# First attention with rows loaded already turned, its mean folded into the query weights and its body in another order

## The chip, the cores and the metric

The kernel runs on one core of a Trainium2 chip. The metric is the device time of one execution in microseconds (us). A core has five engines with a queue of their own each: TensorE (PE; its weight loads are listed as PEld), VectorE (DVE), ScalarE (ACT), GpSimd (POOL) and SyncE (SP, which here only issues DMAs). They meet through semaphores alone.

## The reference, cut

2048 rows of 512 numbers (32 sequences of 64) go through four blocks, each added to x:

```python
x = x + L0_xattn(layernorm(x), ctx)        # the block that the change touches
x = x + L0_ffn(layernorm(x))               # sparse FFN
x = x + L1_xattn(layernorm(x), ctx, mask)
x = x + L1_ffn(layernorm(x))
# L0_xattn(text, features):
features_n = rmsnorm(features, fn_w)
Q = rmsnorm(text @ Wq.T + bq, qn_w)
K = rmsnorm(features_n @ Wk.T + bk, kn_w)
attn = softmax(Q @ K.T / sqrt(512))        # over the 64 keys of the same sequence
attended = attn @ features_n
```

## The kernel before, in words

The first attention (`l0_attention`) works on 16 tiles of 128 rows (`NT = 16`, `P = 128`); a tile holds two sequences, and `off` masks the other one's keys. `D = 512` lies in `KD = 4` blocks of 128. Each product is made of three fp32r ones, since every operand is split into a high and a low half (`split_mm`, L72, L73, L74): ScalarE writes the high half as a cast, and VectorE or GpSimd subtracts it from the original for the low one. A projection is thus 12 products of 512 columns, the scores 12 of 128, and the attend product 3 of 512.

Before and beside the tiles, the same function prepares the sparse FFN: maxima, scales and splits of its weights w1 and w2 (`w1_largest` in tiles 1 to 4, `scale_w1` and `split_w1` in tiles 7 to 14, `w2_largest`), the small factors c1 and c2 (`split_c1`, `split_c2`), and the layer norm, transposes and splits of the FFN's first 512 rows (`NORM_AT`, `PREP_AT`: one part in each of tiles 11 to 14).

Nothing is scheduled by a planner. Each engine has a list of steps of its own (`sp_steps`, `pool_steps`, `act_steps`, `dve_steps`, `pe_steps`): a hand-written prologue, and then `run`, which calls that engine's `body(n)` for n = 0 to 15. `body(0)` has `first`, `body(14)` lacks `ahead` (nothing of tile n+2), `body(15)` lacks `project` too. An engine executes its list strictly in order, and each step waits for semaphores.

A tile goes through these steps; the lines are those of the kernel before:

- SyncE loads x (L297), the context already turned (`cT_raw`, L302) and the context's rows (`craw`, L307).
- VectorE takes the mean and variance of the rows (L631, L635). GpSimd makes reciprocal square roots: in the prologue by L370 and L372, from then on three at once in `tile_roots` (L391, L393; L397 makes the shift -mean/std). ScalarE normalises the rows (L495). TensorE turns them (L808, four transposes into `bxT`), ScalarE casts the high half (L505), VectorE subtracts for the low half (L639).
- GpSimd weighs the context by `fn_w` (`weigh`, L365), ScalarE casts it (L501) and GpSimd subtracts (`features_lo`, L402). Of the turned context ScalarE casts the high half (L511), and GpSimd subtracts (`features_T`, L407).
- TensorE projects keys and queries. VectorE adds their biases (`key_bias`, L644; `query_bias`, L648); ScalarE squares and sums them (L519, L527; L486 for the context). `key_root` on GpSimd gives `krs`, and VectorE scales the keys into `kn` (`scale_keys`, L652).
- TensorE turns queries (L832) and keys (L838); ScalarE casts, VectorE subtracts (`qk_T`, L656 and L658). Then come the scores, VectorE's scaling with mask (L677) and the row maximum (L679), ScalarE's exponential with the denominator (L570), TensorE's transpose of the probabilities (L891), their split (L577, L691), the attend product, and VectorE's division and residual (`attended`, L664; the reciprocal is L687).

In the trace many of these buffers show as parts of `a_wide` (`xn`, `cw`, `kn`, `qb`, `kb`, the raw turned context) and `a_big` (all high and low halves). TensorE's `body(n)` is: both projections of tile n+1, scores of n, row transposes of n+2, attend of n-1, query and key transposes of n+1, (FFN rows,) probability transpose of n. On GpSimd `body(n)` has this piece, whose wait L423 is spoken of below:

```python
            if project:
                key_root(n + 1)
                pool.wait_ge(s_kn, n + 2)
            ...
            if project:
                features_lo(n + 1)
            if ahead:
                weigh(n + 2)
```

In the last tile TensorE also has products of the FFN's c1 as filler. The FFN's own products follow from 177.84 us on (L1336 and L72 to L74 with `xT_hi`; VectorE's L1213 to L1231, GpSimd's L1082, L1089 and L1095 belong to it). The two later blocks are not touched.

Of the kernel before, what the change touches and what calls it, by code (L numbers as in the profile page):

```python
# [21 lines left out]
ALU = mybir.AluOpType  # L22
# [162 lines left out]
def l0_attention(nc, ctx, big_ctx, m, prep, fw, a):  # L185
# [9 lines left out]
    bq_bank, bk_bank, bxT, b_prep, bqT, bkT, b_s, b_att = m.bank  # L195
    b_pT = b_s[:, P:2 * P]
# [9 lines left out]
    wide = sb("wide", [P, 7 * D])  # L206
    xn, cw, kn, qb, kb = (wide[:, n * D:(n + 1) * D] for n in range(5))
# [17 lines left out]
    nmx, den, rden = sb("nmx", [P, 1]), sb("den", [P, 1]), sb("rden", [P, 1])  # L225
# [14 lines left out]
    x_in, c_in_, cT_in = sem("x_in"), sem("ctx_in"), sem("ctxT_in")  # L240
# [16 lines left out]
    w2_in, s_w2m = [sem("w2_in0"), sem("w2_in1")], sem("w2_max_steps")  # L257

# [16 lines left out]
    LOAD_AT = {2: 2, 3: 3, 4: 0, 5: 1, 10: 2, 12: 3}  # L275
# [17 lines left out]
    def sp_steps(sp):  # L293
# [14 lines left out]

# [2352 lines left out]
```

## Time and profile before

| | us |
|---|---|
| three runs | 1509.44, 1509.60, 1510.46 (median 1509.6) |
| profiled execution, its own time | 1511.27 |
| span of that execution in the trace | 1509.5 |
| TensorE busy | 1463.2 (97%) |
| VectorE busy | 1127.8 (75%) |
| ScalarE busy | 795.1 (53%) |
| GpSimd busy | 710.3 (47%) |
| first attention, up to the FFN's first product | 177.84 |

All times in the text are of the one profiled execution. "Granted clock" is the share of full speed that TensorE was allowed in a stretch. A tile's stretch in the first attention runs from the first product of one key projection to that of the next: the projection of tile 2 begins at 48.25 us, and the stretch from there is called tile 2.

### The profile page before, as it was taken

To read this page: it belongs to the slowest core of one execution; us is meant where nothing else is said; L and a number is where in the kernel's file an instruction comes from. 1 tells how busy PE (TensorE), PEld (TensorE's weight loads), DVE (VectorE), ACT (ScalarE), POOL (GpSimd) and SP (SyncE) were. 2 spreads that over 40 slices of the span, in tenths; PEclk is the share of its full clock that TensorE was granted. 3 is DMA by queue.
4 is the path that set the end of the run, shared out by engine and by line. 5 is a ranking of instruction groups with operands and counts; after the bars stand their busy time and mean duration, and the time that the engine had idled before them with its cause. 6 is when DMAs were issued, how large, how long until landed. Compare 5 with 4: busy or idle time off the path is not lost.

```text
span 1509.5 us, 27579 instructions
## 1 busy us (share of the span) xinstructions
PE 1463.2 (97%) x9895; PEld 846.4 (56%) x9895; DVE 1127.8 (75%) x2172; ACT 795.1 (53%) x3201; POOL 710.3 (47%) x668
## 2 busy tenths in 40 slices
PE   5999999999999799999999999999999999999998
PEld 4888745555555455555555555555565555555554
DVE  5788787878876888776776676677677677667868
ACT  5678841211223576556546654754664565565763
POOL 5668875454565353334334343433434333343553
PEclk9999999999999999999999999999999999999999
DMA  7454435333344565653553554455445445334622
GB/s 248 147 175 136 123 81 126 98 77 50 65 88 72 117 147 84 110 119 64 100 105 53 95 88 81 86 87 95 81 80 105 79 73 103 64 60 67 99 50 112
DMA packets 358936, 146.87 MB, mean 97 GB/s; under 512 B 342304, under 2 KB 342688, under 8 KB 356112
## 3 DMA queue, kind: packets, MB, share of 16 engines
q1 hardware_dynamic: 357504, 137.77, 45.1%
q10 hardware_dynamic: 1296, 7.34, 1.5%
q8 instruction: 78, 1.28, 0.4%
q14 instruction: 58, 0.48, 0.1%
HBM read 58.02 MB, written 4.19 MB: 41 GB/s over the span
## 4 chain that ended last, share of the span: by engine, by line
PE 55%; DVE 5%; ACT 3%; DMA 1%; POOL 1%; issue 1%; SPq 0%; DVEq 0%; POOLq 0%; ACTq 0%
PE bank L72 18%; PE bank L74 17%; PE bank L73 17%; PE bank L2439 3%; ACT a_prob L1836 2%; DMA a_pT_lo<-a_p_lo 1%; POOL a_prob L1707 1%; DVE a_oT_lo L2106 1%; DVE x_res L2193 1%; DVE a_qve L2045 1%; ACT a_oT_lo L1813 0%; DVE a_p_lo L2094 0%; DVE a_nmx L2082 0%; DVE a_qr_lo L2035 0%; POOL a_xr_lo L1731 0%
## 5 line engine op out<-in xcount | busy, mean ns | idle before, releaser
L1836 ACT ACTIVATE a_prob<-a_prob,a_nmx 128x64 f32<-128x64 f32 x512 | 170.2, 334 | 183.7 <-DVE a_nmx L2082 183.7
L72 PE MATMUL bank<-w,a_oT_hi 128*128 128x512 f16 x512 | 194.0, 379 | 1.8 <-DVE a_oT_lo L2106 0.9
L74 PE MATMUL bank<-w,a_oT_hi 128*128 128x512 f16 x512 | 194.0, 379 | 0.0
L73 PE MATMUL bank<-w,a_oT_lo 128*128 128x512 f16 x512 | 194.0, 379 | 0.0
L72 PE MATMUL bank<-w,xT_hi 128*128 128x448 f16 (+1 forms) x512 | 188.0, 367 | 3.1 <-DVE h L1231 2.0
L73 PE MATMUL bank<-w,xT_lo 128*128 128x448 f16 (+1 forms) x512 | 187.7, 367 | 0.0
L74 PE MATMUL bank<-w,xT_hi 128*128 128x448 f16 (+1 forms) x512 | 187.5, 366 | 0.0
L1707 POOL TENSOR_TENSOR a_prob<-a_prob,a_mask 128x512 f32<-128x512 f32 x64 | 79.8, 1268 | 204.5 <-DVE a_prob L2076 204.5
L2031 DVE SCALAR_TENSOR_TENSOR x_res<-bank,a_oinv,x_res 128x512 f32<-128x512 f32 x128 | 95.5, 746 | 75.0 <-PE bank L74 75.0
L1157 ACT CAST f_h_hi<-h 128x448 f16<-128x448 f32 x64 | 35.6, 563 | 209.7 <-DVE h L1231 209.6
L1719 POOL TENSOR_TENSOR a_krs<-a_kve,neg_half 128x4 f32<-128x4 f32 x32 | 32.8, 1026 | 239.6 <-DVE a_kve L2056 239.6
L1813 ACT ACTIVATE a_oT_lo<-bank 128x128 bf16<-128x128 f32 x512 | 134.1, 292 | 0.0
L2035 DVE SCALAR_TENSOR_TENSOR a_qr_lo<-bank,a_qr_hi 128x512 f16<-128x512 f32 x128 | 87.9, 687 | 52.2 <-ACT a_oT_lo L1813 51.1
L1713 POOL TENSOR_TENSOR a_p_hi<-a_prob,a_rden 128x512 f16<-128x512 f32 x64 | 69.8, 1090 | 107.3 <-DVE a_rden L2090 107.3
L1095 POOL TENSOR_TENSOR f_h_lo<-h,f_h_hi 128x448 f16<-128x448 f32 x64 | 72.7, 1140 | 91.0 <-ACT f_h_hi L1157 91.0
L1813 ACT ACTIVATION_READ_ACCUMULATOR a_oT_lo<-bank 128x1 f32 x512 | 115.3, 228 | 0.0
L1724 POOL TENSOR_TENSOR a_qrs<-a_qve,neg_half 128x8 f32<-128x8 f32 x64 | 105.3, 1663 | 2.8
L72 PE MATMUL bank<-w,a_cT_hi 128*128 128x256 f16 x384 | 104.9, 273 | 1.1 <-DVE a_qr_lo L2035 1.0
L74 PE MATMUL bank<-w,a_cT_hi 128*128 128x256 f16 x384 | 104.7, 273 | 0.0
L73 PE MATMUL bank<-w,a_cT_lo 128*128 128x256 f16 x384 | 104.7, 273 | 0.0
L72 PE MATMUL bank<-w,a_xT_hi 128*128 128x512 f16 x256 | 97.0, 379 | 0.0
L73 PE MATMUL bank<-w,a_xT_lo 128*128 128x512 f16 x256 | 97.0, 379 | 0.0
(351 smaller groups left out, 4120.5 us busy)
## 6 DMA issues: line engine op xcount, KB each, us to landing
shared<-in_l_wq SPq DMA_DIRECT2D x8, 1024.0 KB, 5.0
shared<-in_l_wo SPq DMA_DIRECT2D x8, 1024.0 KB, 5.1
shared<-in_w ACTq DMA_DIRECT2D x8, 896.0 KB, 4.7
craw<-in_w SPq DMA_DIRECT2D x11, 512.0 KB, 3.9
a_wide<-in_l_ctxT SPq DMA_DIRECT2D x16, 256.0 KB, 4.0
x_res<-in_x SPq DMA_DIRECT2D x16, 256.0 KB, 4.5
shared<-in_ctx SPq DMA_DIRECT2D x16, 256.0 KB, 4.4
shared<-in_l_wkv SPq DMA_DIRECT2D x8, 512.0 KB, 3.9
```

The lines of the kernel that those rows point to most:

```text
L72: pe.matmul(out, a_hi, b_hi, start=first, stop=False)
L73: pe.matmul(out, a_lo, b_hi, start=False, stop=False)
L74: return pe.matmul(out, a_hi, b_lo, start=False, stop=last)
L1095: pool.tensor_tensor(h_lo[:, quarter(q)], h[:, quarter(q)], h_hi[:, quarter(q)], ALU.subtract).then_inc(s_hl, 1)
L1707: pool.tensor_tensor(blocks(prob[u][:, :]), blocks(prob[u][:, :]), mask[:, :].unsqueeze(1).broadcast_to([P, NB, S]), ALU.add).then_inc(s_m ...
L1713: pool.tensor_tensor(blocks(p_hi[u][:, :]), blocks(prob[u][:, :]), share, ALU.mult).then_inc(s_ph, 1)
L1724: pool.tensor_tensor(qrs[:, half], qve[:, half], m.neg_half[:, half], ALU.pow).then_inc(s_qrs, 1)
L1813: ins = act.activation(squares[:, t * G + h, :], q_banks[t][:, h * HD:(h + 1) * HD], ACT.Square, scale=SUM_DOWN, accum_out=qss[:, h % 2, t ...
L1836: ins = act.activation(pt, pt, ACT.Exp, bias=nmx[:, col:col + 1], accum_out=den[:, col:col + 1])
L2031: dve.scalar_tensor_tensor(xt, banks[t % 2][:, :], oinv[:, c:c + 1], xt, ALU.mult, ALU.add).then_inc(s_x, 1)
L2035: dve.scalar_tensor_tensor(qr_lo[:, t, :], q_banks[t][:, :], SUM_DOWN, qr_hi[:, t, :], ALU.mult, ALU.subtract).then_inc(s_ql, 1)
L2439: ins = pe.matmul(pv_banks[u][b][:, cols], v[rows, 2 * u + t, :], p[u][rows, cols], start=n == 0, stop=n == 2)
```

## The change

**Rows.** The host lays x out turned as well (`l0_xT`, like `l0_ctxT`). SyncE loads it into two buffers `xT_raw` (256 KB a tile; the region `wide` grows from 7 to 8 times 512 columns). ScalarE casts the high half out of it (`rows_T`). The low half is made by GpSimd for tiles 0 to 7 (`POOL_ROWS = 8`) and by VectorE for tiles 8 to 15, now out of SBUF instead of a bank. ScalarE's `normalise`, the four row transposes of TensorE, the bank `bxT` and GpSimd's shift (L378, L397) are gone.

**Layer norm.** The projection takes raw rows. The mean is taken out of the weights: Wq minus the mean over its input dimension. In the prologue GpSimd adds two pairs of blocks of Wq (`add_wq`), VectorE adds the two sums, TensorE multiplies that by a matrix of 1/512 (one plain f32 product of 512 columns into `bkT`), and VectorE subtracts the result from the four blocks (`centre_wq`) before they are split. The 1/std of a row is applied in `query_bias`, which becomes a three-operand form like `key_bias`.

**Order.** All five lists are rewritten. TensorE's `body(n)` is now: keys projection of n+1, key transposes of n, probability transpose of n-1, query projection of n+1, scores of n, attend of n-1, query transposes of n+1 (, FFN rows). In tile 14 both transposes stand together and attend(13) behind them. `attended` on VectorE moves one tile later (n-2), and so `rden` and `sums` are doubled. GpSimd's wait for the scaled keys is gone. The transposed maxima of w1 and w2 move from the scores' bank to others. SyncE's order of loads and the tiles at which w1's pieces are loaded change a little.

The core of the diff:

```diff
@@ sp_steps @@
+        def load_xT(n):
+            if n:
+                sp.wait_ge(xT_in, n * 16)
+            sp.dma_start(xT_raw[n % 2][:, :, :], a.l0_xT[n]).then_inc(xT_in, 16)
...
-            if n + 2 < NT:
-                load_x(n + 2)
+            if n + 1 < NT:
+                load_x(n + 1)
+            sp.wait_ge(s_xTl, n - 1)
+            load_xT(n)
@@ pool_steps @@
+        def add_wq(out, half):
+            pool.wait_ge(wq_in[half], 16)
+            pool.tensor_tensor(out, w_raw[0][:, 2 * half, :], w_raw[0][:, 2 * half + 1, :], ALU.add).then_inc(s_mean, 1)
+        def rows_T(n):
+            pool.wait_ge(s_xTh, n + 1)
+            pool.tensor_tensor(xT_lo[:, :, :], xT_raw[n % 2][:, :, :], xT_hi[:, :, :], ALU.subtract).then_inc(s_xTl, 1)
         def body(n, first=False, ahead=True, project=True):
+            features_lo(n)
+            if project:
+                weigh(n + 1)
             tile_roots(n)
             if ahead:
                 features_T(n + 2)
             if project:
                 key_root(n + 1)
-                pool.wait_ge(s_kn, n + 2)
...
-            if project:
-                features_lo(n + 1)
-            if ahead:
-                weigh(n + 2)
-            if n - 1 in SPLIT_AT and n != NT - 2:
+            if ahead and n + 2 < POOL_ROWS:
+                rows_T(n + 2)
+            if n - 1 in SPLIT_AT:
                 split_w1(SPLIT_AT[n - 1])
@@ act_steps @@
-        def normalise(n):
...
         def rows_T(n):
-            act.wait_ge(s_xT, n + 1)
-            act.copy(xT_hi[:, :, :], blk(bxT)).then_inc(s_xTh, 1)
+            act.wait_ge(xT_in, (n + 1) * 16)
+            if n:
+                act.wait_ge(s_q, n)
+            act.copy(xT_hi[:, :, :], xT_raw[n % 2][:, :, :]).then_inc(s_xTh, 1)
@@ dve_steps @@
         def rows_T(n):
-            dve.tensor_tensor(xT_lo[:, :, :], blk(bxT), xT_hi[:, :, :], ALU.subtract).then_inc(s_xTl, 1)
+            dve.scalar_tensor_tensor(xT_lo[:, :, :], xT_raw[n % 2][:, :, :], 1.0, xT_hi[:, :, :], ALU.mult, ALU.subtract)\
+                .then_inc(s_xTl, 1)
         def query_bias(n):
             dve.wait_ge(s_q, n + 1)
-            dve.tensor_tensor(qb[:, :], bq_bank[:, :], bq, ALU.add).then_inc(s_qb, 1)
+            wait_rows_root(dve, n)
+            if n:
+                dve.wait_ge(s_qss, n)
+            dve.scalar_tensor_tensor(qb[:, :], bq_bank[:, :], rs(n), bq, ALU.mult, ALU.add).then_inc(s_qb, 1)
+        def centre_wq(k):
+            dve.tensor_tensor(w_raw[0][:, k, :], w_raw[0][:, k, :], w_mean[:, :], ALU.subtract).then_inc(s_mean, 1)
@@ pe_steps @@
-        def rows_T(n):
-            pe.wait_ge(s_xn, n + 1)
-            for k in range(KD):
-                ins = pe.transpose(bxT[:, k * P:(k + 1) * P], xn[:, k * P:(k + 1) * P], m.ident[:, :])
-            ins.then_inc(s_xT, 1)
...
         def body(n, first=False, ahead=True, project=True):
             if project and not first:
+                pe.wait_ge(s_kb, n + 1)
                 project_k(n + 1)
+            if n != NT - 1:
+                k_T(n)
+            if not first:
+                probs_T(n - 1)
+            if project:
                 project_q(n + 1)
...
-            if ahead:
-                rows_T(n + 2)
-            if not first:
+            if not first and n != NT - 2:
                 attend(n - 1)
             if project:
                 q_T(n + 1)
+            if n == NT - 2:
                 k_T(n + 1)
...
+            if n == NT - 2:
+                attend(n - 1)
...
         project_k(0, first=True)
-        rows_T(0)
-        project_q(0, first=True)
+        pe.wait_ge(s_mean, 3)
+        pe.matmul(w_mean[:, :], thin[:, :], w_sum, start=True, stop=True).then_inc(s_mean, 1)
         pe.wait_ge(s_kb, 1)
         project_k(1)
+        project_q(0, first=True)
         q_T(0)
-        k_T(0)
-        rows_T(1)
```

In the changed kernel the lines are others: L872 turns the queries, L878 the keys, L898 the FFN's rows; on VectorE L674 scales the keys, L655 is the row split, L663 and L670 the key and query biases, L678 and L682 the query and key splits, L686 the probability split, L703 `attended`.

**TensorE, end of one tile and start of the next, before** (middle tiles): bank 6 holds scores and turned probabilities, bank 1 keys, bank 0 queries, bank 7 the attend product, banks 2, 4 and 5 the turned rows, queries and keys.

```order
L74 MATMUL bank6<-a0_big 128x128
L808 MATMUL bank2<-ident,a0_wide 128x128 x4
L72 MATMUL bank7<-a0_big,a0_pT_hi 128x512
L73 MATMUL bank7<-a0_big,a0_pT_lo 128x512
L74 MATMUL bank7<-a0_big,a0_pT_hi 128x512
L832 MATMUL bank4<-ident,a0_wide 128x128 x4
L838 MATMUL bank5<-ident,a0_wide 128x128 x4
L891 MATMUL bank6<-ident,a0_prob 128x128
L72 MATMUL bank1<-a0_big 128x512
```

The key transposes (L838) follow the query transposes (L832) directly.

**TensorE there, after:** from the last product of the scores to the first of the next key projection, and the end of that projection.

```order
L74 MATMUL bank6<-a0_big 128x128
L72 MATMUL bank7<-a0_big,a0_pT_hi 128x512
L73 MATMUL bank7<-a0_big,a0_pT_lo 128x512
L74 MATMUL bank7<-a0_big,a0_pT_hi 128x512
L872 MATMUL bank4<-ident,a0_wide 128x128 x4
L72 MATMUL bank1<-a0_big 128x512
...
L74 MATMUL bank1<-a0_big 128x512
L878 MATMUL bank5<-ident,a0_wide 128x128 x4
L891 MATMUL bank6<-ident,a0_prob 128x128
L72 MATMUL bank0<-a0_big 128x512
```

The row transposes L808 are gone, and the key transposes and the probability transpose moved behind the next tile's key projection (bank 1), directly before the query projection (bank 0).

**VectorE, a middle tile (tile 9), before**, from the key bias to the splits of the turned queries and keys; the banks are those above, and `a0_wide` and `a0_big` lie in SBUF:

```order
L644 SCALAR_TENSOR_TENSOR a0_wide<-bank1,a0_root4,shared 128x512
L631 BN_STATS a0_ln_st<-x_res 128x6
L635 BN_AGGR a0_sums<-a0_ln_st 128x2
L648 TENSOR_TENSOR a0_wide<-bank0,shared 128x512
L677 SCALAR_TENSOR_TENSOR a0_prob<-bank6,a0_root4,a0_off 128x128
L679 TENSOR_REDUCE a0_nmx<-a0_prob 128x1
L652 SCALAR_TENSOR_TENSOR a0_wide<-a0_wide,a0_krs,shared 128x512
L639 TENSOR_TENSOR a0_big<-bank2,a0_big 128x4x128
L664 SCALAR_TENSOR_TENSOR x_res<-bank7,a0_rden,x_res 128x512
L687 RECIPROCAL a0_rden<-a0_den 128x1
L656 TENSOR_TENSOR a0_big<-bank4,a0_big 128x4x128
L658 TENSOR_TENSOR a0_big<-bank5,a0_big 128x4x128
```

The residual of tile n-1 (L664) stands between the row split (L639) and the two splits.

**VectorE there, after,** from the head of the tile to its scaled keys:

```order
L703 SCALAR_TENSOR_TENSOR x_res<-bank7,a0_rden,x_res 128x512
L697 RECIPROCAL a0_rden<-a0_den 128x1
L678 TENSOR_TENSOR a0_big<-bank4,a0_big 128x4x128
L663 SCALAR_TENSOR_TENSOR a0_wide<-bank1,a0_root4,shared 128x512
L682 TENSOR_TENSOR a0_big<-bank5,a0_big 128x4x128
L686 SCALAR_TENSOR_TENSOR a0_pT_lo<-bank6,a0_root4,a0_pT_hi 128x128
L647 BN_STATS a0_ln_st<-x_res 128x6
L651 BN_AGGR a0_sums<-a0_ln_st 128x2
L670 SCALAR_TENSOR_TENSOR a0_wide<-bank0,a0_root4,shared 128x512
L728 SCALAR_TENSOR_TENSOR a0_prob<-bank6,a0_root4,a0_off 128x128
L730 TENSOR_REDUCE a0_nmx<-a0_prob 128x1
L674 SCALAR_TENSOR_TENSOR a0_wide<-a0_wide,a0_krs,shared 128x512
```

The residual (L664, now L703) moved to the head of the tile and belongs to the tile before last; the query split and key split, once a pair, stand around the next key bias; the row split now stands behind the scaled keys and reads `a0_wide` (SBUF) instead of bank 2.

**TensorE, end of tile 14 and start of tile 15, before:** the attend product, the turned queries, keys and FFN rows, the probabilities, and the scores of tile 15 (only their first product is shown).

```order
L74 MATMUL bank6<-a0_big 128x128
L72 MATMUL bank7<-a0_big,a0_pT_hi 128x512
L73 MATMUL bank7<-a0_big,a0_pT_lo 128x512
L74 MATMUL bank7<-a0_big,a0_pT_hi 128x512
L832 MATMUL bank4<-ident,a0_wide 128x128 x4
L838 MATMUL bank5<-ident,a0_wide 128x128 x4
L878 MATMUL bank3<-ident,xln 128x128 x4
L891 MATMUL bank6<-ident,a0_prob 128x128
L72 MATMUL bank6<-a0_big 128x128
```

The attend product stands ahead of all transposes.

**TensorE there, after:**

```order
L74 MATMUL bank6<-a0_big 128x128
L872 MATMUL bank4<-ident,a0_wide 128x128 x4
L878 MATMUL bank5<-ident,a0_wide 128x128 x4
L898 MATMUL bank3<-ident,xln 128x128 x4
L72 MATMUL bank7<-a0_big,a0_pT_hi 128x512
L73 MATMUL bank7<-a0_big,a0_pT_lo 128x512
L74 MATMUL bank7<-a0_big,a0_pT_hi 128x512
L891 MATMUL bank6<-ident,a0_prob 128x128
L72 MATMUL bank6<-a0_big 128x128
```

The attend product moved behind all transposes of tile 14, and the probability transpose behind it; the keys' transposes stay ahead of the scores.

## Rows read from the trace of the kernel before

**Rows 1.** page, part 1: busy us (share of the span) and instructions

```profile
PE 1463.2 (97%) x9895; PEld 846.4 (56%) x9895; DVE 1127.8 (75%) x2172; ACT 795.1 (53%) x3201; POOL 710.3 (47%) x668
```

**Rows 2.** stretches: length, busy us PE PEld DVE ACT POOL, clock, DMA share, GB/s

```profile
0.00:36.90 36.90, 20.56 (x89) 15.30 (x90) 18.61 (x37) 18.74 (x37) 21.02 (x39) 0.98 0.77 250
36.90:48.25 11.35, 11.35 (x54) 9.50 (x53) 4.89 (x11) 5.86 (x15) 5.46 (x9) 0.78 0.35 84
48.25:161.59 113.34, 110.24 (x643) 94.56 (x641) 97.18 (x189) 89.49 (x203) 84.85 (x106) 1.00 0.50 163
161.59:177.84 16.25, 14.88 (x87) 11.71 (x85) 11.26 (x28) 12.50 (x27) 13.99 (x17) 1.00 0.33 92
30.00:35.00 5.00, 1.44 (x9) 0.84 (x8) 2.00 (x5) 3.15 (x9) 4.50 (x8) 1.00 0.49 158
35.00:36.00 1.00, 0.08 (x1) 0.08 (x2) 0.89 (x2) 0.85 (x2) 0.13 (x2) 0.58 0.92 167
```

**Rows 3.** timeline, TensorE: start us, us, engine, line, operation, out<-in

```profile
100.52 0.62 PE L808 MATMUL bank<-ident,a_wide 128*128 128x128 f32 x4
100.90 0.48 PE L72 MATMUL bank<-a_big,a_pT_hi 128*128 128x512 f32 x1
```

**Rows 4.** TensorE by line, tiles 2-13: count | busy, mean ns | idle

```profile
L838 PE MATMUL bank<-ident,a_wide 128*128 128x128 f32 x50 | 8.2, 285 | 3.1 <-DVE a_wide L652 3.0
```

**Rows 5.** stretches of tiles 4 and 7 to 13, columns as in rows 2

```profile
66.12:75.06 8.94, 8.94 (x55) 7.74 (x54) 8.19 (x15) 6.04 (x16) 5.91 (x9) 1.00 0.74 249
...
93.66:103.74 10.08, 9.11 (x54) 7.74 (x53) 8.37 (x17) 9.54 (x20) 6.83 (x10) 1.00 0.39 131
103.74:113.38 9.64, 9.14 (x55) 7.75 (x54) 8.00 (x17) 7.70 (x17) 8.03 (x10) 1.00 0.42 139
113.38:122.57 9.19, 9.11 (x55) 7.75 (x54) 8.63 (x23) 7.49 (x17) 7.73 (x10) 1.00 0.29 86
122.57:132.90 10.33, 9.10 (x54) 7.74 (x53) 7.76 (x16) 7.86 (x18) 8.89 (x12) 1.00 0.56 179
132.90:142.44 9.54, 9.54 (x59) 8.18 (x58) 7.64 (x16) 8.64 (x19) 8.18 (x10) 1.00 0.63 207
142.44:151.94 9.50, 9.50 (x59) 8.18 (x57) 7.37 (x14) 8.92 (x20) 7.76 (x10) 1.00 0.19 55
151.94:161.56 9.62, 9.62 (x60) 8.29 (x58) 7.94 (x16) 9.04 (x20) 7.89 (x10) 1.00 0.62 206
```

**Rows 6.** VectorE by line, tiles 2 to 13, columns as in rows 4

```profile
L639 DVE TENSOR_TENSOR a_big<-bank,a_big 128x512 fp32r<-128x512 f32 x13 | 9.0, 690 | 3.4 <-ACT a_big L505 3.4
L644 DVE SCALAR_TENSOR_TENSOR a_wide<-bank,a_root,shared 128x512 f32<-128x512 f32 x12 | 8.9, 742 | 0.0
...
L648 DVE TENSOR_TENSOR a_wide<-bank,shared 128x512 f32<-128x512 f32 x12 | 8.0, 668 | 1.8 <-PE bank L74 1.8
```

**Rows 7.** timeline, head, during VectorE's splits of Wk

```profile
10.61 1.38 DVE L773 SCALAR_TENSOR_TENSOR a_big<-x_res,a_fnw_T,a_big 128x512 fp32r<-128x512 f32 x2
10.79 0.59 POOL L370 TENSOR_SCALAR a_first_rs<-a_first_mv 128x1 f32<-128x1 f32 x1 [5.17 <-DVE a_first_mv L635]
```

**Rows 8.** FFN: timeline, then one line's durations, ns min/median/max

```profile
184.24 2.51 POOL L1089 TENSOR_TENSOR f_w_lo<-shared,f_w_hi 128x1024 f16<-128x1024 f32 x1
...
185.98 1.26 DVE L1225 TENSOR_TENSOR a_wide<-a_wide 128x448 bf16<-128x448 bf16 x1
...
L1225 DVE TENSOR_TENSOR a_wide<-a_wide x46: 624/626/1259, 184.0 to 395.9; 128x448 bf16<-128x448 bf16 x46
```

**Rows 9.** two lines in all tiles, durations ns min/median/max

```profile
L652 DVE SCALAR_TENSOR_TENSOR a_wide<-a_wide,a_krs,shared x16: 741/748/754, 20.6 to 168.0; 128x512 f32<-128x512 f32 x16
...
L402 POOL TENSOR_TENSOR a_big<-a_wide,a_big x16: 1277/1290/1299, 28.7 to 170.6; 128x512 fp32r<-128x512 f32 x16
```

**Rows 10.** timeline, TensorE, last wait of the head

```profile
35.92 1.12 PE L838 MATMUL bank<-ident,a_wide 128*128 128x128 f32 x4 [1.43 <-DVE a_wide L652]
```

**Rows 11.** timeline, TensorE, first product of tile 15's scores

```profile
172.14 0.30 PE L72 MATMUL bank<-a_big 128*128 128x128 f32 x1 [1.37 <-DVE a_pT_lo L691]
```

More of the change, by code:

```diff
@@ L446, in pool_steps @@
         features_T(0)
-        first_row_root(0)
+        add_wq(w_sum, 0)
+        add_wq(w_high, 1)
         first_features_root(0)
         features_T(1)
+        rows_T(0)
         key_root(0)
+        first_row_root(0)
+        weigh(0)
         first_features_root(1)
+        rows_T(1)
         first_row_root(1)
-        weigh(0)
-        first_row_root(2)
-        features_lo(0)
-        weigh(1)
         pool.wait_ge(s_eps, 1)
@@ L663, in attended @@
             xt = m.x[:, bass.ts(n, D)]
[L664 removed]
+            dve.scalar_tensor_tensor(xt, b_att[:, :], rden[:, n % 2:n % 2 + 1], xt, ALU.mult, ALU.add).then_inc(s_x, 1)
         def body(n, first=False, ahead=True, project=True):
[L667 to L670 removed]
+            if n >= 2:
+                attended(n - 2)
+            if not first:
+                denominator(n - 1)
+            q_T(n)
+            if n == 6:
+                w1_scales()
+            if n == NT - 2:
+                w2_scales()
+            if project and not first:
+                key_bias(n + 1)
+            k_T(n)
+            if n - 1 in PREP_AT and n == NT - 1:
+                first_rows_T(PREP_AT[n - 1])
+            if not first:
+                probs_T(n - 1)
+            if n + 3 < NT:
+                statistics(n + 3)
             if project:
                 query_bias(n + 1)
[L673 to L674 removed]
             dve.wait_ge(s_s, n + 1)
@@ L843, in attend, with probs_T, first_rows_T @@
             pe.wait_ge(s_fl, n + 1)
-            pe.wait_ge(s_rden, n + 1)
+            if n:
+                pe.wait_ge(s_x, n)
             row = bass.ts(n % F_RING, D)
             split_mm(pe, b_att[:, :], pT_hi[:, :], pT_lo[:, :], f_hi[:, row], f_lo[:, row], True, True).then_inc(s_att, 1)
+        def probs_T(n):
+            pe.wait_ge(s_p, n + 1)
+            pe.transpose(b_pT, prob[:, :], m.ident[:, :]).then_inc(s_pT, 1)
+        def first_rows_T(t):
+            pe.wait_ge(prep.norm, 1) if t == TPC - 1 else pe.wait_ge(s_n0, t + 1)
+            if t:
+                pe.wait_ge(prep.lo, t)
+            for k in range(KD):
+                ins = pe.transpose(b_prep[:, k * P:(k + 1) * P], m.xln[:, t, k * P:(k + 1) * P], m.ident[:, :])
+            ins.then_inc(prep.ps, 1)
         def body(n, first=False, ahead=True, project=True):
             if project and not first:
+                pe.wait_ge(s_kb, n + 1)
                 project_k(n + 1)
+            if n != NT - 1:
+                k_T(n)
+            if not first:
+                probs_T(n - 1)
+            if project:
                 project_q(n + 1)
@@ L2628 @@
         "l0_ctxT": ctx_rows.reshape(NT, P, KD, P).transpose(0, 3, 2, 1),
+        "l0_xT": given["x"].reshape(NT, P, KD, P).transpose(0, 3, 2, 1),
         "l0_fnwT": given["L0_xattn_fn_w"].reshape(KD, P).T,
```

283 lines of the change are left out of this document (132 added, 151 removed).

## The prediction

> **What bounds the kernel now.** Read the busy shares first [rows 1]: TensorE has 97% of the span, every other engine less, so the time is TensorE's work plus the few places where it waits. Next the first attention cut into stretches [rows 2]: a head up to 36.90 us, tile 1 up to 48.25, tiles 2 to 13 in 113.34 us, and a tail (tiles 14 and 15) up to 177.84, where the sparse FFN's products begin. The head has 20.56 us of TensorE work in 36.90, so 16 us of waits; tiles 2 to 13 have 3.1 us of idle time in 113.34; the tail has 1.4 in 16.25. Tile 1 runs at a granted clock of 0.78 of full speed: TensorE was busy for 1.44 us between 30 and 35 us, and the clock fell at 35. Last, TensorE's operations in tiles 2 to 13 grouped by line [rows 4]: the transposes of the keys (L838) wait for the scaled keys (L652) for 3.1 us in all, and every other line there has 0. Behind the attention everything is TensorE's too, and the change leaves it alone, so I take what the attention gains or loses to reach the end.
>
> **TensorE's work.** The change drops the four L808 transposes of each tile. Start to start they cost 100.90 - 100.52 = 0.38 us [rows 3], so a tile without waits goes from 8.94 us [rows 5] to 8.56, and to 9.0 in tiles 11 to 13, where the FFN's rows are turned as well. The key transposes move behind the next tile's key projection. Between the end of a key projection and its transposes stood the query projection, scores, three transpose groups and the attend product; now stands nearly a whole tile, so the 3.1 us [rows 4] should go.
>
> **What is late next.** Between the key transposes and the scores only one projection remains (twelve products of 0.23 us, 2.7 us) where two stood. In it ScalarE must cast (0.59) and VectorE subtract (0.68) the keys, then the probabilities (0.38 and 0.34, both short): about 2 us, if both engines are free. So VectorE's own backlog decides. Its busy time before is 8.19 us in tile 4 and 8.37, 8.00, 8.63, 7.76, 7.64, 7.37 and 7.94 in tiles 7 to 13 [rows 5]. The change takes off L639 (0.69), adds 0.07 because the query bias becomes a three-operand form (L648 0.67 to L644's 0.74, [rows 6]), and from tile 7 on gives VectorE the row split back from SBUF, for which I take L652's 0.75 [rows 9]. That makes 7.6 in tile 4, and 8.5, 8.1, 8.75, 7.9, 7.8, 7.5 and 8.1 in tiles 7 to 13: below TensorE's 8.56 or 9.0 but for tile 9. Where VectorE's own work is all, TensorE waits 0.2 us in tile 9 and no more. One further wait has another cause: after tile 6 ScalarE splits the FFN's small weights, which gave tile 7 ScalarE work of 9.54 us in a stretch of 10.08 [rows 5]; less the 0.80 of the normalisation it still makes the key cast late, and I take 9.8 us for that tile. Together tiles 2 to 13 would take 105.5 us, 7.9 less than 113.34.
>
> **GpSimd against VectorE.** VectorE operations with two SBUF operands and GpSimd operations delay each other here. In the head a GpSimd operation on a single column that falls into VectorE's weight splits takes 0.59 us [rows 7]; I read most of it as waiting. In the FFN a VectorE operation with two SBUF operands (L1225) takes 0.63 us in the median of 46, and 1.26 where it begins at 185.98, while a GpSimd subtraction runs to 184.24 + 2.51 = 186.75 [rows 8]: of the 0.77 us of overlap it loses 0.63. So they take turns. The kernel before never pays this in a tile: its one such operation, L652, stays between 741 and 754 ns [rows 9], because GpSimd waits for it (the s_kn wait ahead of features_lo). The change removes that wait and puts GpSimd's split or features_lo under it, and from tile 6 on adds a second such operation (the row split). Each GpSimd operation there is 1.29 us [rows 9] or, for the weight split, 1.9. Bounds for what VectorE loses in a tile from 8 on: 0, if they never meet, and 2.5, if both operations wait out a whole GpSimd operation. I take 1.5: the second follows the first directly, and so meets the GpSimd operation that waited its turn (some 1.2 us), and the first meets the tail of one. In tiles 2 to 5 only one such operation is there and VectorE has 1 us to spare; I take 0.6, which costs 0.5 in tile 5 alone (the w1 maxima). Then VectorE's sums make tiles 8 to 13 9.6, 10.25, 9.4, 9.3, 9.0 and 9.6, and tiles 2 to 13 110.2 us, **3.1 less** than before.
>
> The Trainium skill ("SBUF — State Buffer", section "SBUF: two separate sides") says that such a VectorE operation and a GpSimd operation that reads SBUF lock each other out for the whole instruction. The trace's loss of 0.63 in an overlap of 0.77 nearly agrees. By the rule in full the 1.2 above would be 1.3, and six tiles would take 0.6 us more.
>
> **The head.** Before, tile 1 begins at 36.90 after waits of which the last, for the scaled keys, ends at 35.92 [rows 10]. Now Wq is centred by its column mean. Worked forward from the durations of the same operations: first key projection done at 14.1 as before; GpSimd adds the halves of Wq by 13.6, VectorE adds the two sums by 14.4, then comes one plain f32 product of 512 columns for the mean. No row shows that form; the transposes of as many f32 columns take 0.38 us and the first products of the kernel 0.43 at the slower of the two clocks, so I bound it by nothing and by 1.7, four times the latter. It lies beside the statistics on VectorE until 16.2, so I cost it at nothing; uncovered it is at most 1.7. Then eight VectorE operations (four centrings, four splits, 0.61 apart) with ScalarE's casts between end near 21.6, or 23 with the turns of the last paragraph. The second key projection runs in this time, the first query projection ends near 23.5, and the chain query bias, statistics, first_row_root, then GpSimd's features_lo, weigh, tile_roots and features_T (1.29 + 1.29 + 1.15 + 1.3) releases tile 1's key projection at 31.3 without turns and 33 with them. I take 32.8. Tile 1 then takes 8.6 us at full clock or 11.35 as before; TensorE is busy for about 2 us in the 5 before it, little more than the 1.44 after which it fell, so I take the middle, 9.9. Tile 2 begins at 42.7 instead of 48.25: **5.5 less** (bounds 3 and 8.2).
>
> Loads: the turned rows add 256 KB a tile. Tile 4 has all loads together at a DMA share of 0.74 [rows 5]; they are asked for a tile ahead, so I cost them at nothing; uncovered, one late landing is a microsecond.
>
> **The tail.** In tile 14 the scaled keys of tile 15 were computed ahead of the scores' VectorE work; now they stand behind it (0.35 + 0.29 + 0.75 and latency), so the key transposes wait 1.1 us. VectorE then begins tile 15 with the residual of tile 13, which needs the attend product that now stands last in tile 14 on TensorE; only behind it come the query split, key split, FFN-row split and probabilities (0.75 + 0.1 + 0.6 + 0.6 + 0.65 + 0.3), so tile 15's scores wait about 3.1 us, where they wait 1.37 now [rows 11]. 1.1 + 3.1 - 1.4 + 0.4 for work moved to this side of the boundary, less the transposes that were never there, is 3.1 more; with one turn on the keys **3.4 more** (bounds 3 and 4.3).
>
> **Sum.** 5.5 + 3.1 - 3.4 = 5.2 us less. The profiled execution took 1511.3 us for a span of 1509.5; it would take 1506.1. The runs shown have a median of 1509.6, so I predict **1504.4**.
>
> **Rivals.** (1) They hardly meet: GpSimd's operations fall beside those of VectorE that read PSUM. For it: in the tiles before, features_lo kept its 1.28 to 1.30 us [rows 9]; against it: there a wait kept them apart. Head 8.2, tiles 7.9, tail -3.1: 13 less, 1496.6. (2) Slower: VectorE becomes the bound from tile 8 on because both its two-operand operations wait out a full GpSimd operation (2.5 us a tile). Tiles 2 to 13 then take about 118.5 us (5 more), the head gains 3.5 and the tail loses 4.3: 1515. It decides from 2.2 us a tile; rows 8 show a turn of 0.63 for one operation, under a GpSimd operation already well advanced. (3) The gain is there and given back at the FFN's start, where GpSimd splits w2 (L1089, 2.5 us each [rows 8]) without a pause: if its queue is no earlier than now, TensorE waits there for what it gained: 1509.6. Against it: GpSimd loses its last weight split's wait in the tail.
>
> **Chances.** Forecast 0.45 (1501 to 1509), rival 1 0.2, rival 3 0.2, rival 2 0.15. The range from 1496 to 1512 takes in the middle of rival 1 and leaves out half of rival 2 and little else. A measurement of this kernel can tell about 0.2%, 3 us. Faster than 1506.6: rival 1 and some 0.35 of the forecast, 0.55; within 0.2%: 0.3; slower: 0.15.
>
> **What would show it.** L878 (key transposes) without a wait and L872 (query transposes) without one in tiles 2 to 6; scaled keys (L674) and the row split (L655) longer than 0.75 us in tiles 8 to 13, by 1.5 us together; TensorE waiting there for the key or probability split (L682, L686); key projection of tile 2 near 42.7 us; before tile 15's scores a wait of 3 us. Wrong if L674 and L655 stay at 0.75, if the clock keeps to full speed in tile 1, or if a DMA stands as a releaser in tiles 2 to 5.

## The result, and the profile after

The changed kernel is slower. In 20 runs of each, the medians are 1514.96 us against 1509.12, a ratio of 1.0037 (95% interval 1.0029 to 1.0046), or 5.8 us more. I had predicted 1504.4, and a range up to 1512.0: wrong in sign. The time is that of the rival on the slower side (1515), but, as shown below, only in part for its reason.

Busy shares after, the first part of the page, against [rows 1]:

```profile
PE 1463.4 (97%) x9833; PEld 842.1 (56%) x9833; DVE 1144.2 (76%) x2169; ACT 786.4 (52%) x3185; POOL 724.0 (48%) x658
```

TensorE has 62 recorded matmuls fewer and the same busy time. VectorE has three operations fewer and 16.4 us more. Both say: less work, done slower.

First a correction of names. What the text ahead calls "tile n" of a stretch is `body(n)`, whose first product is the key projection of tile n+1 (at 48.25 us that is tile 3's). The stretches are the same; I write "body" from here on. In the kernel after they are, as in [rows 2] (columns: stretch; length; busy PE, PEld, DVE, ACT, POOL; granted clock; DMA share; GB/s):

```profile
0.00:30.46 30.46, 18.36 (x74) 13.12 (x75) 18.98 (x34) 17.45 (x36) 22.91 (x36) 1.00 0.78 269
30.46:38.98 8.52, 8.52 (x49) 7.30 (x49) 6.28 (x12) 4.46 (x11) 8.04 (x11) 1.00 1.09 248
38.98:157.50 118.52, 109.81 (x595) 90.64 (x592) 110.90 (x186) 83.96 (x194) 95.96 (x100) 0.98 0.59 191
157.50:181.09 23.59, 19.15 (x91) 14.76 (x89) 12.41 (x29) 12.11 (x25) 14.36 (x15) 0.83 0.26 84
172.40:181.09 8.69, 8.69 (x32) 6.14 (x32) 1.81 (x5) 1.37 (x5) 2.68 (x4) 0.62 0.28 94
```

| stretch | before | predicted | after |
|---|---|---|---|
| head, up to body 1 | 36.90 | 32.8 | 30.46 |
| body 1 | 11.35 | 9.9 | 8.52 |
| bodies 2 to 13 | 113.34 | 110.2 | 118.52 |
| tail, up to the FFN | 16.25 | 19.7 | 23.59 |
| FFN begins at | 177.84 | 172.6 | 181.09 |

Behind the FFN's start the spans have 1331.7 us before (1509.5 - 177.84) and 1331.2 after (1512.3 - 181.09), so the attention's loss reaches the end. The profiled pair differs by 3.6 us in its own times (1511.27 and 1514.84) and the medians by 5.8; one reason may be the clock in body 1, below.

TensorE's operations in bodies 2 to 13 by line, against [rows 4]:

```profile
L72 PE MATMUL bank<-a_big 128*128 128x512 f32 (+1 forms) x145 | 54.4, 375 | 8.7 <-DVE a_pT_lo L686 8.5
...
L872 PE MATMUL bank<-ident,a_wide 128*128 128x128 f32 x51 | 8.6, 295 | 0.0
L878 PE MATMUL bank<-ident,a_wide 128*128 128x128 f32 x48 | 7.2, 271 | 0.0
```

The transposes wait for nothing, as forecast. The scores (the second shape in the L72 group) wait 8.7 us instead, 8.5 of them for VectorE's probability split (L686), which comes directly behind its key split (L682). The durations of the two VectorE operations with two SBUF operands, against L652's 741 to 754 ns in [rows 9]:

```profile
L674 DVE SCALAR_TENSOR_TENSOR a_wide<-a_wide,a_krs,shared x16: 742/1520/2172, 21.5 to 166.2; 128x512 f32<-128x512 f32 x16
```

```profile
L655 DVE SCALAR_TENSOR_TENSOR a_big<-a_wide,a_big x8: 682/1778/1789, 85.6 to 156.4; 128x512 fp32r<-128x512 f32 x8
```

The timeline of both engines around them shows how it comes about (the end of body 8; ScalarE's rows lie between):

```profile
103.42 1.90 POOL L459 TENSOR_TENSOR w<-shared,w 128x896 f16<-128x896 f32 x1
...
105.18 0.74 DVE L674 SCALAR_TENSOR_TENSOR a_wide<-a_wide,a_krs,shared 128x512 f32<-128x512 f32 x1
105.28 1.78 POOL L417 TENSOR_TENSOR a_big<-a_wide,a_big 128x512 fp32r<-128x512 f32 x1
...
105.84 1.76 DVE L655 SCALAR_TENSOR_TENSOR a_big<-a_wide,a_big 128x512 fp32r<-128x512 f32 x1
```

VectorE scales the keys first; GpSimd's low half of the features (L417, 1.29 us when alone) begins 0.1 us later and ends at 107.06, 0.5 late. VectorE's row split begins at 105.84 and is done at 107.60, 0.54 us behind that end, where it takes 0.68 when alone. So each waited for the other once, to within 0.15 us of a whole operation.

### The profile page after: what moved, and what is told of

The parts are those of the page before. It is cut to its first block, busy times and chain, and to the rows that moved or that the text cites. A ratio compares the mean times of both kernels' runs of the same rounds, so it can differ in the third digit from the quotient of the medians.

```text
span 1512.3 us, 27439 instructions
## 1 busy us (share of the span) xinstructions
PE 1463.4 (97%) x9833; PEld 842.1 (56%) x9833; DVE 1144.2 (76%) x2169; ACT 786.4 (52%) x3185; POOL 724.0 (48%) x658
## 4 chain that ended last, share of the span: by engine, by line
PE 56%; DVE 5%; ACT 3%; DMA 1%; POOL 1%; issue 1%; SPq 0%; DVEq 0%; POOLq 0%; ACTq 0%
PE bank L72 18%; PE bank L73 17%; PE bank L74 17%; PE bank L2484 3%; ACT a_prob L1881 2%; DMA a_pT_lo<-a_p_lo 1%; DVE a_oT_lo L2151 1%; DVE x_res L2238 1%; POOL a_prob L1752 1%; DVE a_qve L2090 0%; DVE a_p_lo L2139 0%; ACT a_oT_lo L1858 0%; DVE x_res L2076 0%; DVE a_qr_lo L2080 0%; POOL a_xr_lo L1776 0%
## 5 line engine op out<-in xcount | busy, mean ns | idle before, releaser
L72 PE MATMUL bank<-w,a_oT_hi 128*128 128x512 f16 x512 | 194.0, 379 | 1.8 <-DVE a_oT_lo L2151 0.9
L72 PE MATMUL bank<-w,xT_hi 128*128 128x448 f16 (+1 forms) x512 | 188.8, 369 | 3.1 <-DVE h L1276 2.0
L72 PE MATMUL bank<-w,a_cT_hi 128*128 128x256 f16 x384 | 104.9, 273 | 1.1 <-DVE a_qr_lo L2080 1.0
L72 PE MATMUL bank<-w,a_xT_hi 128*128 128x512 f16 x256 | 97.0, 379 | 0.0
```

Of the source, the lines that this page charges most:

```text
L72: pe.matmul(out, a_hi, b_hi, start=first, stop=False)
```

## The experiments

All ratios are against runs of the kernel before on the same chip, and so are directly comparable with the 1.0037 of after. The theories: **A**, VectorE and GpSimd take turns over SBUF, and that is what TensorE waits for; **B**, VectorE's own work and order are too long; **C**, the loss is in the tail and its clock; **D** (formed after the first four runs), a part of the waits is ScalarE's. Where two intervals overlap, the difference of the two kernels is not clear of noise, and the text says so.

| kernel | ratio | 95% interval |
|---|---|---|
| after | 1.0037 | 1.0029 to 1.0046 |
| e2, row split from a bank | 1.0005 | 0.9991 to 1.0020 |
| e3, row split and keys from a bank | 0.9982 | 0.9969 to 0.9994 |
| e4, tail in another order | 1.0013 | 1.0000 to 1.0027 |
| e5, before without GpSimd's wait | 1.0065 | 1.0049 to 1.0081 |
| e6, ScalarE scales w1 earlier | 1.0020 | 1.0009 to 1.0032 |
| e1, rows split on GpSimd | 1.0047 | 1.0030 to 1.0063 |
| e11, rows split on VectorE from tile 2 | 1.0049 | 1.0034 to 1.0064 |
| e7, e4 and keys kept in a bank | 0.9967 | 0.9954 to 0.9981 |
| e9, e7 and e6 | 0.9943 | 0.9926 to 0.9959 |
| e10, e9 and rows 8 to 12 through a bank | 0.9939 | 0.9919 to 0.9958 |

**e2 and e3: the same operations with one SBUF operand fewer.**

```diff
+            src = blk(b_top) if n < 15 else xT_raw[n % 2][:, :, :]
-            dve.scalar_tensor_tensor(xT_lo[:, :, :], xT_raw[n % 2][:, :, :], 1.0, xT_hi[:, :, :], ALU.mult, ALU.subtract)
+            dve.scalar_tensor_tensor(xT_lo[:, :, :], src, 1.0, xT_hi[:, :, :], ALU.mult, ALU.subtract)
```

In e3 also:

```diff
+            src = b_top[:, :] if n < 14 else kb[:, :]
-            dve.scalar_tensor_tensor(kn[:, :], kb[:, :], krs[:, :], wqk, ALU.mult, ALU.mult)
+            dve.scalar_tensor_tensor(kn[:, :], src, krs[:, :], wqk, ALU.mult, ALU.mult)
```

> The changed kernel, but VectorE's row split of tiles 8 to 14 takes its first operand from a bank that holds a constant instead of from SBUF: same form, same size, so the same work (0.75 us), but only one SBUF operand; the low halves of these tiles' rows are then wrong. Theory A (VectorE and GpSimd take turns over SBUF, and that is what TensorE waits for): the split falls from 1.78 to about 0.75 us, the scaled keys before it stay near 1.5, the waits before the scores in the bodies of tiles 7 to 13 shrink from 0.8 to 1.6 us each to under 0.5, and the kernel takes 3 to 6 us less than the changed one, at or just below the kernel before. Theory B (VectorE's own work and its new order are too long, whoever else runs): the split keeps VectorE as long, and nothing moves by more than 1 us. Theory C (the loss is all in the tail and its clock): within 1 us too, with shorter waits in the tiles but no shorter time.

> As the run before, and the scaled keys of tiles 0 to 13 also take their first operand from that bank, so no VectorE operation of these tiles has two SBUF operands (the keys of these tiles are then wrong). Theory A: scaled keys and split both take 0.75 us or less, bodies 2 to 12 of TensorE run without waits in 8.6 to 9.0 us each, the stretch of 12 bodies falls from 118.5 to 107 to 109 us, and the kernel takes 9 to 12 us less than the changed one (about 1504). Theory B: the key and probability splits still come late by some tenths a tile from tile 8 on, 114 us or more for the stretch, 1510 or more. Theory C: stretch shorter, time unchanged.

Both came in A's direction; e2 in its range (3 to 6 us), e3 below it (8.3 us where A had 9 to 12). VectorE by line and shape in e3, from 38 to 160 us:

```profile
L687 DVE TENSOR_TENSOR a_big<-bank,a_big 128x512 fp32r<-128x512 f32 x13 | 8.9, 687 | 5.7 <-ACT a_big L548 5.6
...
L679 DVE SCALAR_TENSOR_TENSOR a_wide<-bank,a_krs,shared 128x512 f32<-128x512 f32 x12 | 8.9, 742 | 0.0
...
L658 DVE SCALAR_TENSOR_TENSOR a_big<-bank,a_big 128x512 fp32r<-128x512 f32 x7 | 4.8, 681 | 0.0
L658 DVE SCALAR_TENSOR_TENSOR a_big<-a_wide,a_big 128x512 fp32r<-128x512 f32 x1 | 1.8, 1755 | 0.0
```

The same form takes 681 ns out of a bank in seven tiles and 1755 out of SBUF in the one left as it was. The split's operand is worth 1.0037 - 1.0005 = 0.0032, 4.8 us; the keys' another 0.0023, 3.5 us (the intervals of e2 and e3 just overlap). Together 8.3 us, more than the change lost: without the turns it would have been 2.7 us faster than before. The stretch of 12 bodies fell from 118.5 to 111.35 us, not to the 107 to 109 expected; four waits of 0.8 to 1.6 us stayed, in bodies 7, 9, 11 and 13, and VectorE's idle time ahead of the key split (L687) names ScalarE's key cast, 5.6 us in all. That led to D. (In e2's own profile one body waited 3.65 us, for the same cast behind a late load, which hides the gain in that one execution: 118.50 us.)

**e5: the removed wait alone, in the kernel before.**

```diff
                 key_root(n + 1)
-                pool.wait_ge(s_kn, n + 2)
```

> The kernel before with one part of the change alone: GpSimd's wait for the scaled keys ahead of its low half of the features is gone, all else as it was. Theory A: the scaled keys (L652), between 741 and 754 ns before, take 1 to 2 us in many tiles, since GpSimd now runs under them; VectorE has slack there, so TensorE's wait for the keys grows by 0.5 to 1 us a tile and the kernel takes 3 to 8 us more than before. Theory B (turns are harmless beside VectorE's order): within 1 us, or faster by the 1 to 2 us that GpSimd no longer waits.

This one line costs 9.8 us (0.0065). The scaled keys, and TensorE's wait for them in bodies 2 to 13 (3.1 us before, [rows 4]):

```profile
L651 DVE SCALAR_TENSOR_TENSOR a_wide<-a_wide,a_krs,shared x16: 741/1662/1915, 20.7 to 175.5; 128x512 f32<-128x512 f32 x16
```

```profile
L837 PE MATMUL bank<-ident,a_wide 128*128 128x128 f32 x50 | 8.2, 286 | 8.3 <-DVE a_wide L651 8.3
```

So the wait kept GpSimd from running under the operation that TensorE waited for. A stands, with a loss above the 3 to 8 us that it had; B alone can't explain this, since neither work nor order of VectorE changed here. In the profiled execution the FFN begins 10.0 us later than in the kernel before: 2.0 are lost up to body 2, 5.5 in bodies 2 to 13 (118.86 us, 5.2 of it the wait in the row) and 2.5 in the tail, where the clock fell behind a wait of 1.81 us.

**e4: the tail.** VectorE scales tile 15's keys ahead of the scores' operations, TensorE attends ahead of the transposes, and in tile 15 the probabilities are split before the residual and the FFN rows.

```diff
-            if not first and n != NT - 2:
+            if not first:
                 attend(n - 1)
...
+            if n == NT - 2:
+                scale_keys(n + 1)
             dve.wait_ge(s_s, n + 1)
```

> The changed kernel with its tail in another order and nothing else: in tile 14 VectorE scales the keys of tile 15 ahead of the scores' operations and TensorE does the attend product ahead of all transposes; in tile 15 VectorE and ScalarE split the probabilities before the residual of tile 13 and before the FFN rows. My step on the tail (3.4 us, from these two waits) would give back 3 us. If the clock's fall behind the 2.9 us wait belongs to it (TensorE at 0.62 of full speed from 172.4 to 181.1 us, 3 us lost), it gives back 5 to 7: FFN start near 175 instead of 181, time near 1509. If the FFN's start is set by something else (GpSimd's or ScalarE's weight splits), the FFN starts earlier but waits show up behind it and the time stays within 1 us of the changed kernel.

3.6 us back (1.0037 to 1.0013): more than the 3 of the waits alone, less than the 5 to 7 with the clock. So C holds for a part of the loss. Tail and body 1 in its profile:

```profile
30.39:40.49 10.10, 10.10 (x49) 8.47 (x49) 6.52 (x12) 5.00 (x13) 9.08 (x11) 0.83 1.08 260
...
159.00:176.75 17.75, 15.94 (x91) 12.80 (x89) 12.17 (x29) 11.93 (x25) 12.81 (x13) 0.96 0.20 59
```

The tail took 17.75 us instead of 23.59: 2.6 us fewer of waits (one of 1.81 left) and 3.2 fewer of busy time, at a clock of 0.96 and not 0.83. In this execution the clock fell in body 13, behind a wait of 1.96 us, and not behind the 1.81 in the tail. Body 1, whose code is that of after, took 10.10 us at 0.83 here and 8.52 at 1.00 there. The clock there differs between executions of the same head; the forecast of 9.9 lay between.

**e6: ScalarE.** After has ScalarE scale a piece of w1 early in its list, ahead of the key cast. The row is L570 of after; in the kernel before the same operation (L545) never waited.

```profile
L570 ACT ACTIVATE shared<-shared,a_w_scale x8: 1030/1037/1054, 89.2 to 159.3; 128x896 f32<-128x896 f32 x8
its engine sat idle before it (us, times) until:
  DMA shared<-in_w: 4.2, 2
```

```diff
-            if n in SPLIT_AT:
-                scale_w1(SPLIT_AT[n])
+            if n in LOAD_AT and n >= 6:
+                load_w1(n, LOAD_AT[n])
...
+            if n + 1 in SPLIT_AT:
+                scale_w1(SPLIT_AT[n + 1])
```

> The changed kernel with one thing moved on ScalarE: the scaling of a piece of w1 (1.04 us) is done at the end of the tile before instead of ahead of the key cast, and the last two pieces of w1 are loaded at the head of tiles 10 and 12 instead of at their end. Theory D (part of TensorE's waits in tiles 8 to 13 is ScalarE's: it stands at that operation, 4.2 us in all for the load of w1 in tiles 11 and 13, with the key cast queued behind): the waits ahead of the scores in tiles 7, 9, 11 and 13 shrink by 1 us or more where they have it, ScalarE's wait for the load is gone, and the kernel takes 2 to 4 us less than the changed one. Theory A alone (only VectorE and GpSimd set these waits): the key cast comes earlier, VectorE is no earlier, and the time stays within 1 us of the changed kernel.

1.0020: 2.6 us less than after, though the intervals of the two just overlap. ScalarE's wait for the load is gone, and the wait of body 11 (1.08 us) with it; that of body 13 fell from 1.57 to 0.71. Those of bodies 7, 8 and 10 stayed, and body 9 got one of 1.40. The pair e7 and e9, which differ by this alone, has the same sign and about the same size (0.9967 to 0.9943, 3.6 us; these intervals overlap too), and there the waits of bodies 11 and 13 fell from 1.33 and 1.66 us to nothing and 0.56. D holds for a part: the traces show it, its price is known only roughly.

**e1 and e11: another engine for the row split.** `POOL_ROWS` is 16 in e1 (all on GpSimd) and 2 in e11 (VectorE from tile 2 on).

> The changed kernel with the row split on GpSimd for all tiles instead of only the first 8 (and the wait ahead of c2's split moved behind it). Theory A: VectorE loses 1.78 us a tile from tile 8 on, GpSimd gets 1.29 us more and has 8.9 us of work of its own in a tile of 9; 1 to 4 us less than the changed kernel, with waits now on GpSimd's turned features (key projection). If GpSimd is the bound: 2 to 6 us more than the changed kernel.

> The changed kernel with VectorE doing the row split from tile 2 on instead of tile 8 on, GpSimd relieved of it. VectorE's two-operand operations then meet GpSimd in bodies 1 to 5 as in the later ones: by theory A the split takes 1.0 to 1.8 us there, body 5 (with w1's maxima) waits 3 us or more, bodies 2 to 4 wait 0.5 to 1 us each, and the kernel takes 3 to 7 us more than the changed one (1517 to 1522). If a tile of VectorE has room for it, the same within 1 us.

Both missed. e1 (1.0047) is no faster than after: the split is off VectorE, but its scaled keys now meet a whole GpSimd operation nearly always:

```profile
L674 DVE SCALAR_TENSOR_TENSOR a_wide<-a_wide,a_krs,shared x16: 742/1764/1850, 22.7 to 163.7; 128x512 f32<-128x512 f32 x16
```

Waits of 2.0, 2.1 and 1.5 us stand in bodies 9, 11 and 13 (in the last two ScalarE's wait for the load, 5.0 us in all, comes on top). e11 (1.0049) lost less than expected: about 2 us, inside the intervals. Bodies 2 to 4 waited 0.2 to 0.6 us each, and body 5 1.88, as in after. Moving the split between the two engines gained nothing; taking the operand out of SBUF did.

**e7, e9, e10: whole kernels with fewer turns.** In e7 the keys with their bias (`kb`) of tiles 0 to 13 are written to the free bank 2, in addition to e4's tail. e9 adds e6. e10 also lets ScalarE copy the raw rows of tiles 8 to 12 into the free bank 3 (0.6 us each), from where VectorE splits them.

```diff
-    cw, kn, qb, kb = (wide[:, n * D:(n + 1) * D] for n in range(1, 5))
+    cw, kn, qb, kb_sb = (wide[:, n * D:(n + 1) * D] for n in range(1, 5))
+    kb = lambda n: b_top if n < 14 else kb_sb
```

In e10 also:

```diff
+            act.copy(blk(b_prep), xT_raw[n % 2][:, :, :]).then_inc(s_xTb, 1)
```

> The tail of e4_tail, and the keys with their bias (kb) of tiles 0 to 13 are written to the free bank 2 instead of SBUF, so that the scaled keys read one SBUF operand; the whole is computed. Against e4_tail, theory A: the scaled keys fall to 0.75 us, the row split behind them still takes 1.5 us or more from tile 8 on, no wait in tiles 2 to 6, and 2 to 5 us less than e4_tail: near the kernel before or 3 us below. Theory B: equal to e4_tail within 1 us.

> e7 (tail order, keys in a bank) with ScalarE's order of e6; VectorE's row split of tiles 8 to 15 still has two SBUF operands. It stands between e7 (0.9967 of the kernel before) and e10 (0.9939). If the rest of e10's gain is ScalarE's wait for the load of w1 (4.5 us in e7): 0.9945 to 0.9955, waits in bodies 11 and 13 gone or under 0.5 us. If it is the row split's turns: within 0.0005 of e7, and the waits in bodies 7 to 10 as in e7.

> All of it together, the whole computed: the tail of e4_tail, the keys in a bank, ScalarE's order of e6_scale_early, and for tiles 8 to 12 ScalarE copies the raw turned rows into the free bank 3 (0.6 us more for it), from which VectorE splits them. Theory A with D: tiles 2 to 12 run without waits in 8.6 to 9.0 us each, FFN start near 170 to 172 us, time 1500 to 1504, below both kernels. If A or D falls, it stays within 3 us of the kernel before.

The bank for the keys is worth 6.9 us (e4 to e7), where 2 to 5 were expected: the row split, which was to stay at 1.5 us or more, fell to a mean of 1.21 in e7. ScalarE's order is worth 3.6 (e7 to e9). The rows' bank adds nothing that these runs can tell (0.9943 and 0.9939): with the keys out of SBUF, the split had a median of 1.27 us in e9, and a tile has room for it. e10 takes 1498.8 us, below its forecast of 1500 to 1504. That is 0.61% less than the kernel before, and 16 us less than after by the medians, 14.8 by the ratios. Its stretches:

```profile
0.00:30.35 30.35, 18.43 (x75) 13.08 (x75) 18.96 (x34) 17.43 (x36) 22.79 (x36) 1.00 0.78 269
30.35:38.91 8.56, 8.56 (x49) 7.29 (x49) 5.52 (x12) 4.25 (x11) 7.54 (x11) 1.00 1.10 258
38.91:146.40 107.49, 105.14 (x595) 88.94 (x592) 96.73 (x185) 85.85 (x199) 89.83 (x100) 1.00 0.64 209
146.40:164.75 18.35, 15.97 (x91) 12.22 (x88) 14.62 (x30) 11.90 (x24) 15.33 (x15) 1.00 0.27 86
```

TensorE's busy time for the same work in bodies 2 to 13 is 105.14 us here, at full clock, and 109.81 in after.

## Why the prediction was wrong

The forecast had the FFN begin at 172.6 us, and it began at 181.09. Of these 8.5 us, bodies 2 to 13 have 8.3 and the tail 3.9, and the head with body 1 took 3.7 back. The step that failed is the price of VectorE's lateness on TensorE: the waits of bodies 2 to 13 were put too low, and the slower clock behind a wait was put at nothing there and in the tail, without a reason. So the sum's term of 3.1 us less for these tiles measured 5.2 more, and its 3.4 more for the tail measured 7.3.

**TensorE's work and the transposes' wait: right.** A body without waits takes 8.56 us in e10, as forecast from [rows 3], and the key transposes waited for nothing until the tail.

**The head: right in sign, too small.** 9.3 us gained up to body 2, where I had 5.5 and at most 8.2. The mean product took 1.13 us, within its bound of 1.7, and body 1 began at 30.46: earlier than the 31.3 that my sum gave even without turns. The sum of that chain was too long; no run took it apart. The full clock in tile 1 was one of my signs of being wrong, and it came; but whether body 1 keeps its clock changes from one execution to the next (8.52 us at 1.00 in after, 10.10 at 0.83 in e4), so this part of the gain is luck of the profiled execution, and the middle of 9.9 didn't say so.

**The turns: right in size from body 8 on, too small ahead of it.** Beyond 0.75 us, L674 and L655 together lost 1.0, 2.5, 1.2, 1.2, 1.2 and 1.2 us in bodies 8 to 13, a mean of 1.4 where I took 1.5. I took the first operation for the cheaper one (the tail of GpSimd's) and the second for the whole, and that is how it is (0.2 and 1.03 in four of the six). The pair at the end of body 7, the first to come late, lost 2.1 us (1.84 and 1.78), and body 8 with its wait of 1.59 is behind it. In bodies 2 to 5 I took 0.6; it was 1.05, and ahead of body 5's scores a third operation met GpSimd: VectorE's copy that spreads w1's maxima took 1.29 us,

```profile
L759 DVE COPY wmax_b<-a_w_max x1: 1290/1290/1290, 69.8 to 69.8; 128x256 f32<-128x256 f32 x1
```

against 0.29 us before, though it has one SBUF operand; GpSimd's L422 ran from 69.62 to 70.92 beside it. Body 5 waited 1.89 us where I had 0.5. The Trainium skill ("SBUF — State Buffer", section "Who interferes with whom") names copies among the operations that can take the shared ports; the row agrees, and I had counted operations with two operands only.

**ScalarE's part: missed.** I costed its w1 work at one tile (body 7: 9.8 us forecast, 9.59 measured) and didn't see that the new list puts the scaling ahead of the key cast in eight tiles, and ahead of the load's landing in bodies 11 and 13. e6 and e9 put 2.6 and 3.6 us on it.

**The clock: missed, as large as the waits that I missed.** I let TensorE's clock into the head alone. But a new wait can be followed by a fall. Body 8 (wait 1.59 us) and body 13 (1.57):

```profile
94.87:106.45 11.58, 9.99 (x52) 8.19 (x50) 11.06 (x17) 7.51 (x18) 10.14 (x10) 0.89 0.43 148
106.45:115.50 9.05, 9.05 (x50) 7.57 (x49) 8.68 (x22) 6.92 (x15) 6.94 (x10) 0.95 0.47 156
...
145.47:157.50 12.03, 10.46 (x57) 8.73 (x55) 10.16 (x17) 8.29 (x18) 9.43 (x9) 0.90 0.55 174
```

The wait of body 8 ends at 102.79 and the clock is at half speed from 103.93 to 107.34; that of body 13 ends at 153.35, with half speed from 155.13 to 158.54. The granted shares of these three rows (0.89, 0.95, 0.90) make 2.9 us; all other bodies have 1.00.

Twelve bodies without waits take 9 x 8.56 + 3 x 9.0 = 104.0 us. After has 14.5 more where I had 6.2: 2.9 of clock, and 11.6 behind waits. Only 8.7 of these 11.6 show as idle time, since a body with a short wait loses more than its rows show as idle. Body 3 in after, at full clock:

```profile
48.06:56.96 8.90, 8.78 (x51) 7.22 (x50) 8.61 (x14) 5.53 (x15) 7.18 (x9) 1.00 0.71 226
```

In e10 it took 8.54 us, all of it busy, and at the same clock. So of the 8.3 us missed in bodies 2 to 13, 2.9 are the clock and 5.4 are waits: those of ScalarE and of the turns ahead of body 8. The runs don't part these two cleanly.

More than one execution shows the clock's part. In the 49 runs of the kernel before beside the experiments its mean over the span is 0.9943; in the 20 of after 0.9920, which takes some 3.5 us of full speed away. The five fastest of after (up to 1511.9 us) have 0.9938 and the five slowest (from 1515.8) 0.9894.

**The tail: waits right, the rest missed.** I forecast 1.1 and 3.1 us:

```profile
167.56 0.66 PE L878 MATMUL bank<-ident,a_wide 128*128 128x128 f32 x4 [1.50 <-DVE a_wide L674]
...
172.40 0.45 PE L72 MATMUL bank<-a_big 128*128 128x128 f32 x1 [2.94 <-DVE a_pT_lo L686]
```

Behind the second, the clock stood at 0.62 up to the FFN, one of its two levels (1.2 GHz) for most of the stretch: TensorE's 19.15 us of busy time are 15.97 in e10, so some 3.2 us of clock, an estimate since e10's tail has another order. With about 0.7 more work moved to this side than I had taken, that makes the 7.3 us lost instead of 3.4.

**Rival 2** named 118.5 us for bodies 2 to 13 and 1515, and both came, by luck. Its mechanism, turns of 2.5 us a tile, came in one body of six (9), and by its own numbers it gives 116.2 us and not 118.5. From body 8 on the turns had their forecast size; beside them stood ScalarE's list, the earlier turns, and the clock behind some of the waits. What I should have priced is a wait together with the speed of what follows it. Rival 3 fell: the FFN's start took nothing back (1331.7 and 1331.2 us behind it). Rival 1, in which they hardly meet, is nearest to e10, where the keys' bank and for five tiles the rows' bank keep them apart.

## What to carry to other kernels

A wait that seems to do nothing may keep two engines apart: before removing one, list which operations will then overlap and which of them read SBUF twice. Where VectorE and GpSimd meet, moving the work between them is worth little; a free bank for one operand removed the conflict and gave 6.9 us. Price a new wait on TensorE with the slower clock that may follow it, and treat it as a chance: it differs between executions of one kernel.

## What the runs showed of the hardware

- Turns are whole operations in both directions, to within some 0.15 us: GpSimd's L417, 1.29 us alone, took 1.63 to 1.78 where VectorE's was ahead of it, and VectorE's 0.68 became 1.78 where it came second.
- The clock's answer to a wait isn't fixed. The wait ahead of tile 15's scores is 1.81 us in e9 and in e10. In e9's profile the tail then ran at a mean of 0.84 (19.28 us busy), in e10's at 1.00 (15.97). After's body 5 waited 1.89 us and kept 1.00. In the profiles of after and of the experiments, every fall between body 2 and the FFN began during a wait of 1.2 to 3.7 us or within 2 us behind it; but e1 kept 1.00 behind waits of 2.00 and 2.14 us. Why one wait takes the clock down and a like one doesn't is open; no run here separates it. A single profile of these kernels can thus be some us off the median: after's 20 runs lie between 1509.7 and 1520.5 us.
